# One broadcast multiply per weight slab, and mask-expansion transfers on two queues, in a block-masked attention and LoRA-expert layer

## The reference, cut to what matters

```python
x = L0_attn_data                                  # (2, 4096, 4096) f32
block_mask = mask.reshape(nb, 32, kb, 32).astype(f32).sum(axis=(1, 3)) > 0
elem_mask = repeat(repeat(block_mask, 32, axis=0), 32, axis=1)
x = x + einsum('bsk,nk->bsn', layernorm(x), weight * elem_mask)
z = layernorm(x)
logits = z @ W_router.T                           # 8 experts, top 2, renormalised
h = einsum('nd,erd->ner', z, A) * combine[:, :, None]      # rank 16
x = x + z @ W_base.T + b_base + 2 * einsum('ner,eor->no', h, B)
```

## Time and profile before

| what | us |
|---|---|
| the two times given | 1693.38 and 1805.47, median 1749.43 |
| profiled execution, its own time | 1692.0 |
| its span, slowest core (core 7) | 1690.4 |
| spans of the 8 cores | 1674.2 to 1690.4 |
| PE busy | 1039.3 (61%) |
| DVE busy | 944.2 (56%) |
| mean granted TensorE clock of a core | 0.919 to 0.921 |

### The profile page before, as it was taken

The page is one execution under the profiler, slowest core; times in us unless marked ns, Lnnn a source line. Parts: engine busy times, 40 slices in busy tenths (PEclk is TensorE's granted clock), DMA queues, the critical chain, the costliest instruction groups (busy, mean ns, idle before and its releaser), DMA issues.

```text
span 1690.4 us, 23944 instructions; the slowest of 8 cores (1674.2 to 1690.4 us)
## 1 busy us (share of the span) xinstructions
PE 1039.3 (61%) x8874; PEld 866.5 (51%) x8874; DVE 944.2 (56%) x4736; ACT 9.7 (1%) x26; POOL 32.2 (2%) x48
## 2 busy tenths in 40 slices
PE   0000000110867777777777767007999999999998
PEld 0000000000656666666666666004888888888886
DVE  2566886417989999999999993952001001001001
ACT  0000000000000000000000000000000000000000
POOL 0000000000000000000000000000000000000000
PEclk9999999999988889888898888558999999999999
DMA  9999899214132222222222220575335434534531
GB/s 225 281 272 262 261 291 297 100 18 82 34 68 51 51 51 51 51 51 51 51 51 51 51 51 1 105 140 104 76 76 115 111 76 102 123 76 100 126 76 50
DMA packets 107918, 179.94 MB, mean 106 GB/s; under 512 B 68234, under 2 KB 84762, under 8 KB 103706
## 3 DMA queue, kind: packets, MB, share of 16 engines
q0 software_dynamic: 19792, 77.67, 25.0%
q1 hardware_dynamic: 85706, 67.18, 14.3%
q10 hardware_dynamic: 2304, 33.56, 5.7%
HBM read 222.48 MB, written 16.78 MB: 142 GB/s over the span
## 4 chain that ended last, share of the span: by engine, by line
PE 44%; DVE 31%; DMA 21%; issue 2%; SPq 1%; DVEq 0%; POOL 0%; POOLq 0%; ACTq 0%
PE pp L583 27%; DVE wts L334 21%; PE pp L380 13%; DMA xres<-x_in 8%; DMA wts<-wta 6%; DVE ost L217 4%; DMA packed<-bmt_sb 3%; DMA wts<-mask_in 3%; DVE scr L435 2%; PE pp L597 2%; PE pp L591 2%; DVE scr L248 1%; SPq L145 1%; PE pp L500 1%; DVE xres L348 1%
## 5 line engine op out<-in xcount | busy, mean ns | idle before, releaser
L380 PE MATMUL pp<-wts,xnt 128*128 128x256 bf16 x4096 | 479.9, 283 | 197.7 <-DVE wts L334 197.7
L334 DVE TENSOR_SCALAR wts<-wts,r 128x32 bf16<-128x32 bf16 x4096 | 564.9, 230 | 41.0 <-DMA wts<-wta 40.1
L380 PEld LDWEIGHTS pp<-wts,xnt 128*128 128x128 bf16 x4096 | 414.3, 101 | 263.2 <-issue 201.6
L583 PE MATMUL pp<-wts,xnt 128*128 128x256 bf16 x4096 | 459.7, 276 | 3.0 <-DVE hwt L557 3.0
L583 PEld LDWEIGHTS pp<-wts,xnt 128*128 128x128 bf16 x4096 | 404.4, 99 | 56.2 <-issue 3.5
L613 DVE TENSOR_TENSOR ost<-pp,xres 128x256 f32<-128x256 f32 x128 | 43.9, 416 | 470.8 <-PE pp L597 470.8
L217 DVE TENSOR_REDUCE ost<-wts 128x128 bf16<-128x4096 int32 x32 | 141.4, 4420 | 85.3 <-DMA wts<-mask_in 82.3
L229 PE MATMUL pp<-ost,bd_sb 128*4 128x128 bf16 x32 | 8.5, 265 | 286.8 <-DVE ost L217 286.8
L229 PEld LDWEIGHTS pp<-ost,bd_sb 128*4 128x4 bf16 x32 | 2.6, 80 | 288.6 <-issue 288.6
L348 DVE TENSOR_TENSOR xres<-pp,xres 128x256 bf16<-128x256 f32 x128 | 43.9, 416 | 30.2 <-PE pp L380 27.6
L483 PE MATMUL pp<-wrt,xnt 128*128 128x8 bf16 x256 | 8.0, 168 | 66.8 <-DMA xnt<-xstg 43.6
(11 more groups left out here) (49 smaller groups left out, 129.2 us busy)
## 6 DMA issues: line engine op xcount, KB each, us to landing
wts<-mask_in ACTq DMA_DIRECT2D x16, 2048.0 KB, 11.3
wts<-mask_in SPq DMA_DIRECT2D x16, 2048.0 KB, 11.5
wts<-wta POOLq DMA_DIRECT2D x16, 2048.0 KB, 12.9
wts<-wtb POOLq DMA_DIRECT2D x16, 2048.0 KB, 14.8
y_out<-ost SPq DMA_DIRECT2D x16, 1024.0 KB, 14.0
xres<-x_in POOLq DMA_DIRECT2D x8, 1024.0 KB, 17.8
r<-at_l POOLq DMA_DIRECT2D x1, 1024.0 KB, 8.3
r<-bp_l POOLq DMA_DIRECT2D x1, 1024.0 KB, 10.7
```

The lines of the kernel that those rows point to most:

```text
L334: last = vop(lambda v, kt=kt, j=j, b=b, s=s: v.tensor_scalar(wts[:, b, kt, 32 * j:32 * (j + 1)], wts[:, b, kt, 32 * j:32 * (j + 1)], mexp1 ...
L380: f = (lambda t, kt=kt, tt=tt, b=b, bank=bank, c0=c0, st=st: t.matmul(bank[:, c0:c0 + slab_n], xnt[:, tt, kt, :], wts[:, b, kt, :], start= ...
L583: top(lambda t, kt=kt, tt=tt, b=b, bank=bank: t.matmul(bank[:, 256 * (tt % 2):256 * (tt % 2) + slab_n], xnt[:, tt, kt, :], wts[:, b, kt, : ...
```

## The change

There are two edits. In the mask expansion, the 32 small transfers go by turns to SP's queue (semaphore `sAsm`) and ACT's queue (a new semaphore `sAsm2`), and each waits for the one before it on its own queue. In the attention stage, the 256 multiplies of a slab become one `tensor_tensor` over the whole slab, whose second operand is the mask with each value repeated 32 times by a step of 0. For that `mexp1` becomes bf16, in the first half of `r2`, with the same values 0 and 1.

```diff
@@ -100,6 +100,7 @@
+        sAsm2 = e(nc.semaphore("sAsm2"))
@@ -109,7 +110,7 @@
-        mexp1 = r2[:].bitcast(F32).rearrange("p (a c) -> p a c", a=NKT)
+        mexp1 = r2[:, 0:D].rearrange("p (a c) -> p a c", a=NKT)
@@ -288,11 +289,13 @@
         for kt in range(NKT):
-            w = [(pV, v_bmt)] if kt == 0 else [(sAsm, c_asm[kt - 1])]
-            c_asm.append(dma(RY, sAsm, bmTw[:, NB * kt:NB * (kt + 1)],
+            qs = (kt % 2 == 0)
+            lst, semq = (RY, sAsm) if qs else (RA, sAsm2)
+            w = [(pV, v_bmt)] if kt < 2 else [(semq, c_asm[kt - 2])]
+            c_asm.append(dma(lst, semq, bmTw[:, NB * kt:NB * (kt + 1)],
                              bmt_sb[4 * kt:4 * (kt + 1), :], waits=w))
             bank = pp[3 + (kt % 2)]
-            w = [(sAsm, c_asm[kt])]
+            w = [(semq, c_asm[kt])]
@@ -327,17 +330,12 @@
-            last = None
-            for kt in range(NKT):
-                for j in range(nbs):
-                    tick = (kt == NKT - 1 and j == nbs - 1)
-                    last = vop(lambda v, kt=kt, j=j, b=b, s=s: v.tensor_scalar(
-                        wts[:, b, kt, 32 * j:32 * (j + 1)],
-                        wts[:, b, kt, 32 * j:32 * (j + 1)],
-                        mexp1[:, kt, nbs * s + j:nbs * s + j + 1], None, op0=ALU.mult),
-                        waits=(w if (kt == 0 and j == 0) else ()),
-                        selfw=(kt == 0 and j == 0), tick=tick)
-            return last
+            return vop(lambda v, b=b, s=s: v.tensor_tensor(
+                wts[:, b].rearrange("p a (j r) -> p a j r", r=32),
+                wts[:, b].rearrange("p a (j r) -> p a j r", r=32),
+                mexp1[:, :, nbs * s:nbs * (s + 1)].unsqueeze(3)
+                    .broadcast_to([128, NKT, nbs, 32]),
+                op=ALU.mult), waits=w)
```

## The result

The changed kernel takes 1471.51 us, the median of 12 runs, against 1700.73 us for the kernel before, 10 runs. The ratio is 0.8663, with a 95% interval of 0.864 to 0.8687. The forecast was 1467 us. The profiled execution took 1470.6 us for a span of 1469.0 (core 6, the slowest), which is 221.4 less than the span before; the sum had said 225.4.

What follows compares the result with a forecast made beforehand. The prediction took DVE's L334 multiplies to bound the attention stage, after a latency-bound mask expansion. Savings of 26 (expansion), 26.4 (first multiply) and 173 us (slabs behind) took 1692.0 to 1466.6, forecast 1467 us, range 1450 to 1575.

Steps and rivals of the forecast that it cites:

- The multiply: Attention stage: one multiply per slab on DVE takes 8.9 us, replacing 35.32 us for 256 separate ones.
- the slower rival: Slab multiply keeps a higher fixed price per 32-column run; over 41.3 us makes the kernel 2% slower; chance 0.01.
- the first multiply's place: Ahead of slab 0's matmuls: the shorter first multiply saves 26.4 us.
- The limit of 14.2 us: Attention stage: PE never waits while a slab's multiply stays under 14.2 us, with a load of 12.9.
- The slab: Attention stage: PE becomes the bound at 28.05 us per warm slab; slabs behind the first multiply save 173 us.
- The bound of 25 us: Attention stage: clock dips as in some last-stage slabs cost at most 1.67 us x 15 = 25 us; none taken.
- the 16 different matmuls: Last stage: matmuls of L591 and L597 ahead of the 29.72 us slabs, half on a single row; attention stage lacks them.
- The mask expansion: Before the first slab load: two rows of 16 small transfers side by side take 27.9 us instead of 54.8; -26 taken.
- The first: Rival: slab multiply over 14.2 us, so load, multiply and matmul of one buffer are the cycle; 1513 us; chance 0.07.
- The second: Rival: mask expansion gains nothing since the two queues take turns; 1493 us; chance 0.06.
- The third: Rival: PE at full load on eight cores is not granted its clock; 1679 us, or 1573 as a middle; chance 0.10.
- The fourth: Rival: slower, as the slab multiply costs more per 32-column run than the present instruction; 1763 us at 45 us; chance 0.01.

Runs made afterwards that it cites:

- the run with pairs: Changed kernel with each mask value stored twice side by side, so the slab multiply's second operand steps by one innermost: 1466.69 us, ratio 0.8648.
- one and a half multiplies: Changed kernel with half of each slab multiplied by the mask a second time: 1477.34 us, ratio 0.8692.
- the kernel with everything but the early load: Changed kernel with mask values stored twice, four small transfers in flight, expansion matmuls not waiting for their predecessor's end: 1463.94 us, ratio 0.8601.
- the run with the queues only: Kernel before, with only the small transfers of the mask expansion put by turns on SP's and ACT's queue: 1671.70 us, ratio 0.9839.
- the two early loads: Changed kernel with the first two slab loads released when the block mask is cast: 1469.71 us, ratio 0.8673.
- the single one: Changed kernel, mask values stored twice, four small transfers in flight, no wait between expansion matmuls, slab 0's load alone released at the mask cast: 1451.52 us.

## Why the prediction was right

**What bounds the kernel.** It named the multiplies of L334 in the attention stage as what is waited for last, and the mask expansion as pure latency. Both hold: -200.7 us came from the first multiply and the slabs, -23.1 from the expansion, and the three other places of the table, which the change doesn't touch or hardly, lost 2.5 us.

**The multiply.** It took 8.9 us from two-source rows of other shapes; 8.69 was measured. The estimate by the Trainium skill's rule (Vector Engine (DVE) Microarchitecture Reference, 5.1 Performance modes) was 8.6, and the run with pairs shows that the rule's reason holds too. The other end, a price for each run of 32 columns, is excluded by the same 8.69 us, and with it the slower rival. For the first multiply's place -26.4 was forecast and -26.3 measured, partly by luck: the multiply was 0.2 us shorter than charged and the load 0.3 longer.

**Where PE becomes the bound.** The limit of 14.2 us was a little too high, because it took every load as 12.9 us, the median before. In the changed kernel the median is 13.5:

```profile
wts<-wta POOLq DMA_DIRECT2D x16, 2048.0 KB, 13.5
```

With one and a half multiplies one load took 14.75 us, and 13.2 us of multiplying already showed. At 8.7 us it made no difference. What makes a load longer stays open. A busy PE is not enough: in the kernel with everything but the early load PE works through the stage without a gap too, and the loads' median is 12.7 to 12.9 us on all eight cores.

**The slab.** 28.05 us was charged; slabs come 27.95 us apart. The bound of 25 us for a falling clock was not needed: the stage's clock is 1.00. That fits the guess that the 16 different matmuls have to do with the last stage's 29.72 us, but nothing here tests it, and they can't be the whole cause: there they stand ahead of every slab but the first, and in the changed kernel's chain ten of the 16 slabs take 28.05 us all the same.

**The mask expansion.** -26 was forecast and -23.1 measured in this profile. The forecast charged 16 transfers of 1.67 us and 1.2 behind them. The last small transfer took 3.48 us instead of 1.6, for a reason that no run shows, and two matmuls stood behind it instead of one, 0.6 us more. This is the term that was mis-sized, by 2.9 us. With 1.2 us more at the start and 1.0 at the end that is 5.1; the slabs gave 1.0 back, and about 4 are left between sum and result. The expansion is shorter on the other seven cores, and the run with the queues only puts the term at 26.3 us in the medians. Between the medians of the two kernels lie 227.5 us and not 221.4, so the 4 us are no more than what executions differ by. The term's reason was right in substance and wrong in name: latencies overlap, but a second queue is not needed for it.

**The rivals.** The first (multiply over 14.2 us) did not occur, but doubling the multiply shows that its mechanism is real, at 61.1 us a pair. The second (no gain from the mask expansion) falls by the run with the queues only, where two transfers run side by side and the time is 26.3 us less. The third (no full clock on eight busy cores) does not show in this profile: the granted clock is 0.956 as a mean over the span, 1.00 in the stage and 0.97 in the last one, as before. The fourth falls with the multiply's 8.69 us.

## What to carry to other kernels

Many small in-place instructions on one engine can be the bound of a matmul stage though the page shows neither engine as much as two thirds busy (56% and 61% here); find the relay in the chain, work out how long the middle link may take (here the matmuls of one slab less its load), and check that the new instruction is under that with its real rate. In this kernel a second operand that is repeated by a step of 0 innermost cost 1.04 ns a column even in bf16; storing each value twice halved it, which only pays where that instruction is on the path. For a row of tiny dependent transfers, count how many are in flight and not on how many queues, and start a large load beside them only if they can afford to be nearly four times slower while it runs, as they could with four in flight and one load.

## What the runs showed of the hardware that was not expected

A small SBUF transfer takes 1.6 us alone and up to 6.2 beside slab loads, though it moves 1 KB. Two lines of chains show it, the first beside the two early loads, the second beside the single one:

```profile
331.05 6.23 DMA packed<-bmt_sb
```

```profile
337.53 5.73 DMA packed<-bmt_sb
```

One early load together with four small transfers in flight is a gain of 12.4 us; two early loads with two in flight were none. Matmuls that wait for the semaphore of the one before come 0.62 us apart for 0.26 us of work, and DVE copies with such a wait start 0.17 us after the end of the one before. The 4096 separate multiplies before, which have no such wait within a slab, came 138 ns apart though each shows 230 ns.
